# Reductions of a gated linear attention, four value features at a time on TensorE's column groups; head mean and gate matrices folded into weights

## The reference, cut to what matters

```
k = split(inputs @ Wk * SCALE);  kg = split(inputs @ Wg1 @ Wg2);  v = split(inputs @ Wv)
log_gate = log_sigmoid(kg) / 16
state = state * exp(log_gate)[..., None] + k[..., :, None] * v[..., None, :]   # over 512 tokens
out   = einsum('bhd,bhde->bhe', q, state)                                       # sum over the 8 keys
mu = mean(o, -1); var = var(o, -1); o = (o - mu) * rsqrt(var + EPS)             # over the 16 value features of a head
attn = (silu(inputs @ Wg + bg) * o) @ Wo
```

## Time and profile before

| what | us |
|---|---|
| median of 3 runs (685.5 to 687.59) | 685.81 |
| the profiled execution, its own time | 689.51 |
| its span in the trace | 687.3 |
| TensorE matmuls busy | 552.0 |
| VectorE busy | 439.9 |
| ScalarE busy | 304.7 |
| GpSimd busy | 162.4 |

### The profile page before, as it was taken

One profiled execution on the slowest core, in us unless ns is written; L12 is line 12 of the kernel. 1 busy time (PEld: TensorE's weight loads), 2 busy tenths in 40 slices (PEclk: granted clock), 3 DMA queues, 4 the chain that ended last, 5 costly groups with the idle time before them and its releaser, 6 DMA issues. The chain is left out here.

```text
span 687.3 us, 6312 instructions
## 1 busy us (share of the span) xinstructions
PE 552.0 (80%) x1928; PEld 207.6 (30%) x1928; DVE 439.9 (64%) x675; ACT 304.7 (44%) x509; POOL 162.4 (24%) x177
## 2 busy tenths in 40 slices
PE   4287786878987799999798998888988787886662
PEld 1111132213333221334342223534413343330531
DVE  3279429894537789746769897477666556624224
ACT  2320252221655537363667554354765525665031
POOL 0035425541212233413113342321100010000000
PEclk9778898995999999999999999898979978976666
DMA  4710034260223221122113102001111200000000
GB/s 140 200 32 0 1 46 123 81 134 1 46 32 100 72 76 46 48 47 31 59 46 113 39 9 78 31 17 55 56 60 48 77 0 2 1 2 0 31 0 31
DMA packets 34354, 34.52 MB, mean 50 GB/s; under 512 B 5713, under 2 KB 32017, under 8 KB 34321
## 3 DMA queue, kind: packets, MB, share of 16 engines
q1 hardware_dynamic: 33504, 33.92, 18.3%
q10 hardware_dynamic: 816, 0.20, 0.1%
HBM read 22.37 MB, written 8.39 MB: 45 GB/s over the span
## 5 line engine op out<-in xcount | busy, mean ns | idle before, releaser
L954 DVE TENSOR_REDUCE MX<-bank 128x1 f32<-128x512 f32 x256 | 170.4, 682 | 128.0 <-PE bank L444 127.6
L754 ACT ACTIVATE PT<-bank 128x512 f32<-128x512 f32 x256 | 147.4, 595 | 168.2 <-PE bank L453 159.6
L444 PE MATMUL bank<-KS,QS 96*128 96x512 bf16 x256 | 102.4, 409 | 27.9 <-DVE MX L954 24.1
L1014 POOL TENSOR_TENSOR Pq<-qT,St 128x512 f32<-128x512 f32 x64 | 84.0, 1313 | 159.0 <-DVE St L863 140.0
L453 PE MATMUL bank<-QS,KS 99*128 99x512 bf16 x256 | 103.8, 412 | 19.3 <-ACT PT L754 12.2
L863 DVE TENSOR_TENSOR_SCAN St<-ab,U 128x512 f32<-128x512 f32 x64 | 91.3, 1426 | 1.0
L429 PE MATMUL bank<-Pq,hsel 128*32 128x512 f32 x128 | 75.2, 673 | 13.5 <-POOL Pq L1014 13.1
L467 PE MATMUL bank<-PT,Vs 128*32 128x512 f32 x512 | 78.0, 671 | 0.8 <-ACT PT L754 0.8
L453 PEld LDWEIGHTS bank<-QS,KS 99*128 99x128 bf16 x256 | 25.1, 100 | 111.8 <-issue 61.7
L444 PEld LDWEIGHTS bank<-KS,QS 96*128 96x128 bf16 x256 | 25.4, 100 | 100.6 <-DVE MX L954 57.6
L857 DVE TENSOR_TENSOR U<-kT,bank 128x512 f32<-128x512 f32 x64 | 42.9, 671 | 15.8 <-PE bank L422 15.7
(11 more groups left out here) (119 smaller groups left out, 666.7 us busy)
## 6 DMA issues: line engine op xcount, KB each, us to landing
KS<-k_parts SPq DMA_DIRECT2D x96, 64.0 KB, 2.3
QS<-q_parts SPq DMA_DIRECT2D x96, 64.0 KB, 2.3
VB<-parts SPq DMA_DIRECT2D x24, 128.0 KB
k_parts<-parts SPq DMA_DIRECT2D x12, 256.0 KB, 2.1
q_parts<-parts SPq DMA_DIRECT2D x12, 256.0 KB, 2.3
xT<-in_xT SPq DMA_DIRECT2D x4, 512.0 KB, 3.4
cT<-in_cT SPq DMA_DIRECT2D x4, 512.0 KB, 3.3
xtok<-in_x SPq DMA_DIRECT2D x4, 512.0 KB, 3.9
```

The costliest lines, as they stand in the source:

```text
L444: pe.matmul(bank(n)[:, :], QS[0:NS, h, i * P:(i + 1) * P], KS[0:NS, h, :], start=True, stop=True).then_inc(filled(n), 1)
L754: act.activation(PT[:, n % 2, j, :], bank(name)[:, :], ACT.Exp).then_inc(emptied(name), 1)
L954: dve.tensor_reduce(MX[:, NT * h + i:NT * h + i + 1], bank(n)[:, :], AX.X, ALU.max).then_inc(emptied(n), 1)
L1014: pool.tensor_tensor(Pq[:, e % 2, :], qT[:, :], St[:, e % 2, :], ALU.mult).then_inc(p_done, 1)
```

## The change

1. **Reductions.** `reduce_step` (one feature, 64 in all) becomes `reduce_four`: four matmuls in a row into the four 32-row groups of the bank, 16 groups in all. Which feature goes to which rows is rearranged by `value_feature` in the broadcast matmul. Pq has a ring of 6 tiles in place of 2. Group q waits until feature 4q+3 is multiplied, and stands at quarter 3 of slots 2, 4, 6 and 8 (for stages 0 and 1 the last one at (0, 0) of the next stage).
2. **Head mean.** wv is changed once, at the start, on VectorE: from each column the mean of its head's 16 columns is taken. The mean matmul and the subtraction (L880) go; `var` moves from (2, 2) to (1, 2), the square on ScalarE from (2, 1) to (1, 0), and what follows moves by a step or so.
3. **Gate matrices.** `wkg = wg1 @ wg2` is made once at the start (two matmuls, a ScalarE copy); per batch one projection with wkg at (1, 3) remains. The Abs, Exp, Ln and the VectorE step of the decay move about a step forward.
4. **Room.** x1 is normed straight into x1b, and the bias is added to it in place once the transposes have read it; PT becomes a ring of 6 tiles in place of 8.

The core of the diff:

```
+def value_feature(k):
+    return 8 * (k // 8) + 2 * (k % 4) + k % 8 // 4
...
-            def reduce_step(a, e):
-                g, j, i = e // 8, (e % 8) // 2, e % 2
-                pe.wait_ge(p_done, count(DV, a, e + 1))
-                if e % 8 == 0:
+            def reduce_four(a, q):
+                g, i = q // 2, q % 2
+                pe.wait_ge(p_done, count(DV, a, 4 * q + 4))
+                if i == 0:
                     pe.wait_ge(*free_for(f"o{g}", a))
-                pe.matmul(bank(f"o{g}", a)[32 * j:32 * j + 32, :], hsel[:, i, :], Pq[:, e % 2, :],
-                          start=(i == 0), stop=(i == 1)).then_inc(r_done, 1)
+                for j in range(4):
+                    ins = pe.matmul(bank(f"o{g}", a)[32 * j:32 * j + 32, :], hsel[:, i, :],
+                                    Pq[:, (DV * a + 4 * q + j) % PQN, :], start=(i == 0), stop=(i == 1))
+                ins.then_inc(r_done, 1)
...
-                if 1 <= slot <= DV // 2 and i % 2 == 1:
-                    reduce_step(r, 2 * (slot - 1) + i // 2)
+                if slot in (2, 4, 6, 8) and i == 3:
+                    reduce_four(r, slot // 2 - 1)
...
-                if slot == DV // 2 and at in ((0, 0), (0, 1)):
-                    reduce_step(o, DV - 2 + at[1])
+                if slot == DV // 2 and at == (0, 0):
+                    reduce_four(o, RQ - 1)
...
-                    pool.wait_ge(r_done, count(DV, r, max(e - 1, 0)))
-                    pool.tensor_tensor(Pq[:, e % 2, :], qT[:, :], St[:, e % 2, :], ALU.mult).then_inc(p_done, 1)
+                    k = DV * r + e
+                    if k >= PQN:
+                        pool.wait_ge(r_done, FIRST + (k - PQN) // 4 + 1)
+                    pool.tensor_tensor(Pq[:, k % PQN, :], qT[:, :], St[:, e % 2, :], ALU.mult).then_inc(p_done, 1)
...
-                if at == (2, 0):
-                    dve.wait_ge(*full_of("mean", o))
-                    for g in range(ND):
-                        ins = dve.tensor_tensor(oS[:, g, :], oS[:, g, :], bank("mean")[:, :], ALU.subtract)
-                    ins.then_inc(emptied("mean"), 1)
...
+            by_head = wv[:, :, :].rearrange("p k (h e) -> p (k h) e", e=DV)
+            dve.tensor_reduce(hsum[:, :], by_head, AX.X, ALU.add).then_inc(v_sum, 1)
...
+            dve.scalar_tensor_tensor(by_head, hsum[:, :].unsqueeze(2).broadcast_to([P, ND * H, DV]), -1.0 / DV, by_head,
+                                     ALU.mult, ALU.add).then_inc(cst, 1)
...
+            pe.wait_ge(*free_for("wkg", 0))
+            for k in range(ND):
+                ins = pe.matmul(bank("wkg", 0)[:, k * P:(k + 1) * P], wg1T[:, k * P:(k + 1) * P], wg2[:, :],
+                                start=True, stop=True)
+            ins.then_inc(filled("wkg", 0), 1)
```

More of the change, by code:

```diff
@@ L37 @@
 STEPS = range(-2, B + 2)
+RQ = DV // 4
+PTN = 6
+PQN = 6
 def stages(s):
@@ L99, in use @@
         at[name, batch] = (bank, uses[bank], signals.get(bank, 0))
+    use("wkg", 0, 2)
     for s in STEPS:
@@ L478, in projecting @@
                 if at == (1, 3):
[L479 to L484 removed]
+                    pe.wait_ge(*read("wkg", 0))
+                    by_feature("gg", r, wkg, 0, xT)
                 if at == (3, 0):
```

91 lines of the change are left out of this document (41 added, 50 removed), and 4 rows, old and new, of the table SIDE_USES.

## The result

The changed kernel takes 696.29 us (median of 4 runs, 693.69 to 696.61), the kernel before 686.7 beside it; the ratio is 1.0128, with a 95% interval of 1.0092 to 1.0165. It is slower by 1.3%, some 9 us. The forecast was 677.0 us, faster, with 0.09 for slower: it was wrong in sign. The profiled execution took 696.19 us, 694.4 in the trace; that of before 689.51 and 687.3.

What follows compares the result with a forecast made beforehand. PE was taken to bound only the front halves of stages 0 to 3, balanced with VectorE in their recurrence parts, VectorE pacing stages -2 and -1. Terms summed to -8.8 us off the median 685.81, giving 677.0 us; range 667 to 685.

Steps and rivals of the forecast that it cites:

- What bounds: Recurrence parts of stages 0 and 1: PE and VectorE balanced, VectorE idle only 3.1 and 4.3 us, so PE's savings become waiting.
- The reductions: Sums over keys on PE: a group of four costs what one did, 1.05 us; 48 of 64 go, some 50 us.
- Stage -2 and -1: Recurrences of these stages: VectorE's waits shrink and one instruction moves to an idle place; -1.3, -0.7 and -1.0 us.
- The turn: Stage changes 0 to 1 and 1 to 2: PE waits for GpSimd's product ahead of the value projection; +1.1 us each.
- Front half of stage 0: Head steps 2 and 4 of stage 0: mean matmul and L484 go, an exponential comes sooner; -1.6 and -1.3 us.
- Front halves of stages 1 and 2: Ahead of the recurrence parts: 2.8 us leave PE in stage 1, one matmul of 1.72 in stage 2; -2.0 and -1.7.
- Stages 0 and 1: Recurrence parts: VectorE's idle time falls to 1.0 us in each, -2.1 and -3.3, together -5.4 us.
- The clock: Recurrence parts of stages 0 and 1: an idler PE runs some 15 more us cold, at 0.27 us each; +4 us.
- Slower, by the clock: Rival: gain gone when 47 of the 112 us of stages 0 and 1 run cold, clearly slower from 55; chance 0.09.
- The start: Ahead of the first broadcast: 0 to 3.6 us of added VectorE and PE work, hidden behind VB's transfer; taken as 0.

Runs made afterwards that it cites:

- e4: The changed kernel with the last group of four of the batches of stages 0 and 1 moved behind the next stage's first value projection; 691.07 us.
- e5: e1 with the square, var, inverse deviation and GpSimd's two multiplications back at their old, later quarters; 680.9 us, ratio 0.9905 to the kernel before.
- e6: The changed kernel with the square, var, inverse deviation and GpSimd's two multiplications back at their old, later quarters; 691.27 us, ratio 1.0039 to the kernel before.
- e1: The changed kernel with one reduction per feature again, head mean and gate matrices still folded; 684.55 us, ratio 0.9958 to the kernel before.
- e14: e4 plus 11 unneeded products of the old reductions' form, waiting for nothing, at old reduction places in stage 0; 682.79 us, ratio 0.9875 to the kernel before.
- e13: e12 plus 4 more unneeded products at each of four later places in stage 0; 687.21 us, ratio 0.9959 to the kernel before.
- e16: The changed kernel with single reductions in stages -2 to 0, pairs in stage 1, last pair behind the value projection, square's chain late in stage 2 only; 674.66 us.
- e3: The changed kernel with each of the 64 broadcast products made five times into the same bank; 710.77 us, ratio 1.0342 to the kernel before.
- e7: The changed kernel with 48 unneeded broadcast products in stage 0, ahead of PE's waits for broadcast banks; 698.03 us, ratio 1.0148 to the kernel before.
- e12: e4 plus 16 unneeded products in stage 0, where PE waits just ahead of its first cold stretch; 692.25 us, ratio 1.0043 to the kernel before.

## Why the prediction was wrong

**What bounds.** Right: PE and VectorE are balanced in the recurrence parts, and PE's freed time did not become time won. But VectorE's idle time there, which was to fall under 1.5 us per part, rose to 5.0 and 5.2.

**The reductions.** Right in count and price: 16 groups, 1.06 us at full clock, 1.94 at half. The estimate of 1.4 us from the Trainium skill's tile speed-ups (TensorE: Matmul & The Clock Gate, Measured speedup vs the span model) is not what these rows show.

**"Stage -2 and -1": -3.0; measured -0.5.** The trace shows a granted clock of 0.59 and 0.65 in these two parts after the change, where it was 0.80 and 0.87. The maxima of stage -1 that were to come 1.0 earlier waited 1.71 instead of 1.52 us. The prediction's clock term counted the 112 us of stages 0 and 1 alone; these 85 us were not in it. Not tested by itself.

**"The turn": +1.1 each; by its terms 2.2 in all.** The mechanism was right, the size was not. The wait was 2.98 and 2.41 us, not 1 to 2, since PE was through with the scores of the stage by 283.0; and what the sum left out was that a PE that has waited starts the projection at the lower clock (2.98 us instead of 1.99). Moving the last group of both batches by a quarter gave 5.2 us back by the medians, 6.9 by the traces (e4).

**"Front half of stage 0": -2.9; measured -4.1.** Better than forecast, and for another reason. Head step 2 was to go from 9.5 to 7.9 us with ScalarE's queue as its limit; it took 3.8 (maxima tiles at 182.30 and 186.10), and the query projection came at 187.1 instead of 192.6. 1.6 us of the gain are the clock's: `var` had run at the lower one (3.52 us) and now took 1.88.

**"Front halves of stages 1 and 2: -2.0, -1.7".** This is a step that failed outright in stage 2: with the turn it was to be -0.6 and was +6.3. 3.4 of the 6.3 are the turn's (from the last scan to V0 of stage 3, e4 has 117.4 us and the changed kernel 120.8). For the rest, the step read ScalarE's queue and PE's, and never asked what else the earlier square sets free. It sets free GpSimd's multiplications, and these fell upon VectorE's norm. The same step cost nothing in stage 0, where no norm of a last stage stands there. Putting the chain back is worth some 7 us of stage 2 (e5 and e6), so that the folds, had the chain stayed late there, would have been a gain in it (109.9 us in e5, 114.3 before). The trace of before had the sign of it: the later norm, at 453.9, took 3.30 us beside a multiplication of GpSimd, and 1.38 after the change, without one.

**"Stages 0 and 1: -5.4" and "The clock: +4".** Together -1.4; measured +2.8 and +0.6. The step that failed is "with some 15 more cold us in the 112": it was 45 (27 and 21 against 3). Its price of 0.27 us per cold us (0.31 if 4.3 us doubled are 8.6, and not 8) no run confirms: if the -5.4 was there to be had, which no run shows either, it was (3.4 + 5.4) / 45, 0.20. So a size was off by a factor of three. That alone takes the forecast to about no change, since the prediction itself had put the point where the gain is gone at 47 cold us; slower it became by stage 2, the turns and the gain that stages -2 and -1 did not bring. It had met the rival "Slower, by the clock" with "after such stretches the clock comes back"; it does, but a cold stretch in the part of stage 0 lasts 7 to 10 us in the changed kernel, and there are three of them, where there was one of 3.4 before. The Trainium skill (TensorE: Matmul & The Clock Gate, HAM oscillation — how this bites in real kernels) had it right that a PE which is kept waiting loses its clock again and again; the prediction named this and gave it 0.09.

**The start: 0.** Right. The first projection came 2.1 us later, the first broadcast at 35.39.

**The sum, split by the runs.** Between e1 and the changed kernel lie 11.7 us by the medians and 12.7 by the traces behind V0 of stage 0: the price of the groups of four. e4 gives back 6.9 of the 12.7, the turn's; e14, built on e4, another 6.5, by keeping stage 0 and the front of stage 1 at full clock. That is the whole price and 0.7 more, by one trace each. What the folds bring, 0.4% in e1, would be 1.0% but for GpSimd (e5).

What stays open: which work holds the clock. PE busy for 7.44 of 8 us did not, 5.45 did. Open too is the clock's part in stage 1, where no run put the work back and the lengths hardly follow the clock (57.8 us at 1.00, 58.4 at 0.82), and why executions of one kernel lie 10 us apart in e13 and 17 in e4.

## What to carry to other kernels

Where two engines are balanced, taking work from one is no gain by itself, and when that one is TensorE it can be a loss: look up the granted clock of the stretch, count how many us would run at half of it, and put that price beside the gain ahead of the edit. A wait moved to the head of a stage is paid twice on TensorE, once as wait and once as the slower work behind it; where one place in the order further back is free, use it. When an edit makes a chain start earlier, list every engine that the chain wakes, and ask what those instructions will stand beside; a good stage-by-stage answer (early in three stages, late in the fourth; run only together with pairs, e16) was worth more here than the change that was made.

## What the runs showed of the hardware

**VectorE beside GpSimd.** Four VectorE TENSOR_SCALAR instructions of 128x256 fp32 took 1.38 us with GpSimd still, 2.31 to 2.53 with part of one of its 128x1024 multiplications beside them, 4.69 with most of two (e3), and 6.81 with three in a row, ending with the third. The Trainium skill (SBUF — State Buffer, SBUF: two separate sides) says that the two engines share a pair of ports as an exclusive lock, held for a whole instruction; the trace agrees, with the three long instructions that each end about 0.15 us behind a multiplication, and shows beyond it that VectorE can lose the pair several times in one short group. GpSimd's multiplications kept their 2.34 to 2.37 us beside this group.

**Useful or not, work can buy time on TensorE.** 11 products that nothing reads made the part of stage 0 2.7 us shorter, and 6.5 us in all from V0 of stage 0 on. Of another form (bf16, 48 rows), 10 us in e7 and 3.4 us just ahead of the cold stretch in e12 did not.

**The first transfer's time varies from run to run.** The first broadcast waited for VB until 35.4 us in the changed kernel and 39.1 in e4, with nothing changed ahead of it; over the traces of the kernels that are alike up to there it lay between 34.6 (e13) and 39.6 us (e12). That is 5.0 us, more than most single effects here, and the reason to compare traces from V0 of stage 0 on.
